# Two projection matmuls per step of a Trainium2 attention kernel, issued from slots 13 and 14 instead of slots 2 and 3

## The reference

```python
Q = _split_heads(x @ Wq.T + bq)              # x: (8, 512, 512), 16 heads of 32
K = _split_heads(x @ Wk.T + bk)
V = _split_heads(x @ Wv.T + bv)
tQ = _split_heads(tokens @ Wq.T + bq)        # tokens: one row for each of the 8 batches
tK = _split_heads(tokens @ Wk.T + bk)
cQ = Q + tQ
cK = K + tK
scores = jnp.einsum('bhqd,bhkd->bhqk', cQ, cK) / jnp.sqrt(jnp.float32(HEAD_DIM))
attn = jax.nn.softmax(scores, axis=-1)
out = jnp.einsum('bhqk,bhkd->bhqd', attn, V)
...
x = x + out
```

## Time and profile before

| | |
|---|---|
| median of 3 runs | 644.05 us (643.90 to 644.67) |
| the profiled execution's own time | 645.23 us |
| its span, first to last instruction | 643.4 us |
| PE busy | 636.5 us, 99% |
| PE's weight loads busy | 438.0 us, 68% |
| DVE busy | 543.8 us, 85% |
| POOL busy | 488.1 us, 76% |
| ACT busy | 388.3 us, 60% |
| share of PE in the chain that ended last | 95% |
| granted TensorE clock | full speed (2.4 GHz) in all of the span |

### The profile page before, as it was taken

The page is one execution under the profiler, slowest core; times in us unless marked ns, Lnnn a source line. Parts: engine busy times, 40 slices in busy tenths (PEclk is TensorE's granted clock), DMA queues, the critical chain, the costliest instruction groups (busy, mean ns, idle before and its releaser), DMA issues.

```text
span 643.4 us, 10063 instructions
## 1 busy us (share of the span) xinstructions
PE 636.5 (99%) x3528; PEld 438.0 (68%) x3528; DVE 543.8 (85%) x818; ACT 388.3 (60%) x684; POOL 488.1 (76%) x204
## 2 busy tenths in 40 slices
PE   8999999999999999999999999999999999999997
PEld 6777677666677666677666677666776666776542
DVE  6886888888888888888888888888888888998887
ACT  6465666565566565566565666566666555564773
POOL 6438877778877779877779777779777778666991
PEclk9999999999999999999999999999999999999999
DMA  7944334555334555334555334555344565424501
GB/s 245 270 108 118 105 102 97 146 151 148 99 104 100 147 150 137 101 105 107 149 149 132 104 101 115 150 151 129 102 103 116 149 164 136 116 71 120 144 24 61
DMA packets 48243, 80.83 MB, mean 126 GB/s; under 512 B 9545, under 2 KB 9801, under 8 KB 48073
## 3 DMA queue, kind: packets, MB, share of 16 engines
q1 hardware_dynamic: 47837, 80.04, 47.6%
q10 hardware_dynamic: 356, 0.16, 0.1%
HBM read 19.95 MB, written 8.39 MB: 44 GB/s over the span
## 4 chain that ended last, share of the span: by engine, by line
PE 95%; DVE 2%; issue 1%; DMA 1%; ACT 1%; SPq 0%; POOLq 0%; DVEq 0%; ACTq 0%
PE bank L352 27%; PE bank L445 18%; PE bank L427 18%; PE bank L465 17%; PE bank L400 14%; DMA Pt<-xT 1%; DVE bank L744 1%; ACT Pt L640 1%; DVE part_sums L769 0%; DVE rr L793 0%; DVE ends L814 0%; PE bank L473 0%; DVE rr L782 0%; DVE bank L800 0%; PE bank L377 0%
## 5 line engine op out<-in xcount | busy, mean ns | idle before, releaser
L640 ACT ACTIVATE Pt<-bank 128x512 f32<-128x512 f32 x512 | 299.0, 600 | 207.3 <-PE bank L445 136.0
L744 DVE TENSOR_REDUCE mf<-bank 128x1 f32<-128x512 f32 x496 | 330.7, 684 | 61.8 <-PE bank L427 59.7
L953 POOL TENSOR_TENSOR A<-A,Pt 128x2048 f32<-128x2048 f32 x59 | 271.6, 4603 | 4.6
L427 PE MATMUL bank<-Ks,Qs 128*128 128x512 f32 x496 | 195.9, 396 | 0.2
L445 PE MATMUL bank<-Qs,Ks 128*128 128x512 f32 x496 | 195.4, 400 | 0.1
L953 POOL TENSOR_TENSOR A<-Pt 128x2048 f32<-128x2048 f32 x30 | 138.3, 4608 | 9.3 <-ACT Pt L640 5.0
L445 PEld LDWEIGHTS bank<-Qs,Ks 128*128 128x128 f32 x496 | 92.6, 188 | 48.7 <-ACT Pt L640 26.1
L465 PE MATMUL bank<-Pt,V 128*32 128x512 f32 x1024 | 118.9, 596 | 0.0
L427 PEld LDWEIGHTS bank<-Ks,Qs 128*128 128x128 f32 x496 | 93.0, 187 | 28.4 <-DVE mf L744 6.0
L923 POOL TENSOR_TENSOR Xl<-xr,Xh 128x512 fp32r<-128x512 f32 x28 | 36.3, 1297 | 98.9 <-ACT Xh L601 98.9
L352 PE MATMUL bank<-Xh,Wh 128*128 128x512 f32 x256 | 100.2, 392 | 0.9 <-ACT Xh L587 0.8
(11 more groups left out here) (74 smaller groups left out, 394.0 us busy)
## 6 DMA issues: line engine op xcount, KB each, us to landing
Qs<-hi SPq DMA_DIRECT2D x60, 256.0 KB
Ks<-hi SPq DMA_DIRECT2D x60, 256.0 KB, 3.8
Qs<-lo SPq DMA_DIRECT2D x30, 256.0 KB
Ks<-lo SPq DMA_DIRECT2D x30, 256.0 KB, 3.8
xr<-xT SPq DMA_DIRECT2D x28, 256.0 KB, 2.7
res<-xT SPq DMA_DIRECT2D x28, 256.0 KB, 2.9
outT<-ot SPq DMA_DIRECT2D x28, 256.0 KB, 3.6
Qs<-mt SPq DMA_DIRECT2D x122, 4.0 KB
```

The lines of the kernel that those rows point to most:

```text
L427: e.matmul(MXB[u % 2][:, :], q[:, j, qc * P:(qc + 1) * P], k[:, j, :], start=True, stop=True).then_inc(t_mx, 1)
L640: e.activation(exponentials(g)[:, kc, j, :], st_bank(u)[:, :], ACT.Exp, scale=SCALE).then_inc(a_e, 1)
L744: e.reduce_max(to[:, 4 * j + qc:4 * j + qc + 1], MXB[u % 2][:, :], AXX).then_inc(v_mx, 1)
L953: e.tensor_tensor(sums, ex[:, 0, :, :] if kc == 1 else sums, ex[:, kc, :, :], ALU.add).then_inc(p_a, 1)
```

## The change

In the table of the steps 1 to 24, slots 2 and 3 give one matmul each to slots 13 and 14. The sum stays 36.

```diff
-PROJ = (1, 1, 3, 3, 3, 3, 3, 3, 3, 3, 3, 2, 2, 1, 1, 1)
+PROJ = (1, 1, 2, 2, 3, 3, 3, 3, 3, 3, 3, 2, 2, 2, 2, 1)
```

## The result

| | before | changed |
|---|---|---|
| median of 6 runs | 644.11 us | 650.47 us |
| ratio (95% interval) | 1 | 1.0099 (1.0083 to 1.0114) |
| profiled execution: time, span | 645.23, 643.4 us | 653.22, 651.4 us |
| one step of the loop | 19.38 us | 19.67 us |

The kernel became 6.4 us slower, where 650.8 us and 6.7 us had been forecast. The profiled execution of the changed kernel is the slowest of its six; the other five have spans of 648.3 to 648.9 us. Its own extra lies at the start: the granted clock averaged 0.89 of full speed in its first 10 us, against 1.00 in the kernel before, and its first totals (step 2) come at 78.25 us where they came at 76.70. Of these 1.55 us one changed step explains 0.28. From there on the two traces can be compared.

What follows compares the result with a forecast made beforehand. Taking PE's instruction stream as the bound, the prediction added 0.325 us a step lost at score 7 and subtracted 0.045 gained at slot 14: +0.28 over 24 steps, +6.7 us, from 644.05 to 650.8 us, range 647.7 to 652.9.

Steps and rivals of the forecast that it cites:

- What bounds the kernel: PE's instruction stream, 95% of the span; only waits inside it can change the time, at 19.38 us a step.
- Part 1, the gain: Slots 13 and 14: slot 14's maxima load stops waiting for DVE, gaining 0.045 us a step, 1.1 us in all.
- the DMA traffic: Behind slot 14's maxima: the preferred reading that transfers, which stay in place, cause the 0.233 us spacing instead of 0.227.
- the upper end: Slots 14 to 1: if DVE's wait also causes the wider spacing, the gain is 0.09 us a step, 2.2 us.
- Part 2, the cost: Slots 2 and 3: score 7's load must wait for exp 5, costing 0.325 us a step, 7.8 us in all.
- The second case: Score 7's load runs hidden beside a matmul, so the loss is only 0.20 us a step; 647.8 us, chance 0.06.
- Part 3, the covers: Score 8, DVE, POOL and transfers move at no cost; score 8's bank is free 0.03 us ahead of its load.
- Only the tail counts: Score 7's bank is free when asked, leaving only slot 14's gain: 642.9 us, down to 641.9; chance 0.06.
- Two waits instead of one: Score 8's bank is late as well, making the loss 0.38 us a step, 653.2 us; chance 0.05.

Runs made afterwards that it cites:

- the back part alone: Kernel before with one projection each moved from slots 9 and 10 to slots 13 and 14, slots 0 to 8 unchanged: 642.10 us, ratio 0.9964.
- the front part alone: Kernel before with one projection each moved from slots 2 and 3 to slots 9 and 10, slots 11 to 15 unchanged: 652.54 us, ratio 1.0128.
- one moved: Kernel before with one projection moved from slot 2 to slot 13, nothing else: 645.58 us, ratio 1.0023.

## Why the prediction was right, point by point

**What bounds the kernel.** The stream on PE: confirmed. Every kernel's time follows from the waits inside that stream and the wider spacing behind them; a step without them takes 19.29 us (the back part alone).

**Part 1, the gain.** The mechanism was right, and the wait behind DVE went in the changed kernel and in four experiments. DVE starts on slot 12's maxima 0.79 us behind their matmul in both kernels; what changed is that slot 14's load stands eight instructions behind that matmul instead of seven, and it now comes 0.12 us behind the end of the reduction, where it waited before. The size was taken too low: 0.045 us a step instead of 0.08. The prediction saw one late load in slots 14 to 1, and there are four. Of the two readings of the 0.233 us spacing the prediction preferred the DMA traffic and kept the wait as the upper end (0.09); the back part alone shows the upper end to be the right one.

**Part 2, the cost.** The chain V12, V copy, exp 5, score 7 is what the trace shows, with its terms 0.43, 0.49 and 0.65 us. The price at the wait was 0.31 for 0.325 forecast. The 0.045 us for the instructions behind it, held as an upper bound, is there as well (0.05), so the term measures 0.36. The second case, in which the load is hidden and the price is 0.20, did not come: the load itself waited 0.47 us.

**The two errors together.** Gain and loss were each 0.035 too small, for the same reason (the slower spacing behind a late load, taken for DMA in one place and left out in the other), so their difference of 0.28 us and the 6.7 us came out right. The sum was right partly by this luck; the front part alone and the back part alone show the two terms as 8.4 and 2.1 us, where the prediction's terms were 7.8 and 1.1.

**Part 3, the covers.** Score 8 did not wait, by 0.04 us where 0.03 had been forecast; DVE's and POOL's covers held, no transfer came late. The V copy's wait grew to 1.36 us, as forecast, and the waits in the table became 37.3 us in 64 and 1.7 us in 8 times (about 37 in 64 and 8 forecast). The step became 19.67 us (19.66 forecast).

**The rivals.** "Only the tail counts" describes the experiment with the V copy behind exp 5: with the wait at score 7 removed the kernel is faster than before, by 2.0 us, within the 1.1 to 2.2 forecast for that case. "Two waits instead of one" occurred in none of the kernels looked at.

## What to carry to other kernels

A table that spreads filler work over slots also sets when the last piece of that work ends, and so how soon everything behind it on other engines can run. Ahead of such a change, follow each completion (here the twelfth matmul) through the in-order queue that consumes it to the next buffer that the bound engine asks for, and count the distance in instructions: in this kernel it was 0.02 us from being too short, and nothing in the table of waits showed it. Such near misses show only in the timeline, as the distance from the end of the work that frees a buffer to the load that asks for it. Where the distance is too short, moving the consumer one place back in its own queue can give the gain without the loss.

## What the runs showed of the hardware

- The lateness of a weight load behind a semaphore costs PE the lateness less 0.11 us: 0.20, 0.43 and 0.88 us late lost 0.10, 0.31 and 0.77 us at that place, and 0.16 us late at slot 14 lost 0.045.
- Behind such a wait the next five (one moved) to nine (changed kernel) 128x512 matmuls are spaced about 0.232 us instead of 0.227, also at a DMA share of 0.00. In the one-moved kernel the load of slot 0's maxima, only 0.03 us late, was followed by 0.235. What in PE makes them slower stays open. In slots 14 to 1 of the kernel before, with four late loads, 0.045 us at the first wait became 0.09 in all.
- A DMA share of 0.80 did not slow the stream by an amount that the timeline shows.
